# Scattering the routed rows with four 32-column products side by side instead of four accumulating 128-column products

## The reference, cut to what matters

```python
# L0 ffn, last step: each of 64 slots (16 experts x 4) of a group of 16 tokens goes back to the token that it was picked from
out = jnp.einsum('...besd,...btes->...btd', inter, perm)
# x = x + tanh(g_ffn[0]) * out
# L1 attention, one head, keys and values are ctx_1024
logits = jnp.einsum('bqd,bkd->bqk', q, k) * scale + mask * NEG
attn = jax.nn.softmax(logits, axis=-1)
out = jnp.einsum('bqk,bkd->bqd', attn, v)
# x = x + tanh(g_xattn[1]) * out, then the layer norms of the last feed-forward
```

## Time and profile before

| | us |
|---|---|
| median of 3 runs | 1633.4 (1632.84 to 1636.59) |
| span of the profiled execution | 1630.0 |
| TensorE busy | 1327.1 (81%) |
| VectorE busy | 1032.4 (63%) |
| ScalarE busy | 759.7 (47%) |
| GpSimd busy | 432.6 (27%) |

### The profile page before, as it was taken

The page is one execution under the profiler, slowest core; times in us unless marked ns, Lnnn a source line. Parts: engine busy times, 40 slices in busy tenths (PEclk is TensorE's granted clock), DMA queues, the critical chain, the costliest instruction groups (busy, mean ns, idle before and its releaser), DMA issues. The chain is left out here.

```text
span 1630.0 us, 24926 instructions
## 1 busy us (share of the span) xinstructions
PE 1327.1 (81%) x8930; PEld 934.2 (57%) x8930; DVE 1032.4 (63%) x2374; ACT 759.7 (47%) x1145; POOL 432.6 (27%) x435
## 2 busy tenths in 40 slices
PE   6999999999999738999957999996141799343996
PEld 5787888878888527666524666664041444142442
DVE  5577666766667533444334778786496399776774
ACT  3233333333333212665333555554383655386991
POOL 1233333333323310110012787866100000000011
PEclk9999999999999968999978999998555699755998
DMA  6111222111221158787589988860300177421973
GB/s 217 46 66 67 73 84 103 65 71 66 94 93 40 40 213 293 261 300 271 219 305 278 256 238 231 235 183 29 121 1 3 78 310 305 162 78 51 419 311 149
DMA packets 100406, 261.79 MB, mean 161 GB/s; under 512 B 11120, under 2 KB 22480, under 8 KB 93136
## 3 DMA queue, kind: packets, MB, share of 16 engines
q1 hardware_dynamic: 88704, 226.82, 40.1%
q0 software_dynamic: 8688, 32.51, 5.8%
q10 hardware_dynamic: 2912, 1.14, 0.3%
HBM read 155.32 MB, written 105.12 MB: 160 GB/s over the span
## 5 line engine op out<-in xcount | busy, mean ns | idle before, releaser
L1197 PE MATMUL p_s<-p_rows,p_permT 128*128 128x512 f32 x256 | 131.5, 611 | 5.9 <-DMA p_rows<-inter_d 3.9
L916 PEld LDWEIGHTS p_sel<-p_pick,p_xp 128*128 128x128 bf16 x1536 | 89.5, 100 | 55.5 <-issue 34.2
L916 PE MATMUL p_sel<-p_pick,p_xp 128*128 128x128 bf16 x1536 | 100.9, 224 | 21.9 <-DMA p_xp<-xparts 19.3
L2261 POOL DMA_DIRECT2D p_y<-residual x8 | 10.0, 1254 | 405.4 <-POOLq L113 342.9
L1928 PE MATMUL p_z<-qT,w1T 128*128 128x512 bf16 x512 | 113.3, 385 | 2.1 <-PEq L113 2.1
L1054 DVE COPY p_selT<-p_sel 128x512 f32<-128x512 f32 x64 | 44.2, 691 | 104.5 <-PE p_sel L916 104.5
L2285 PE MATMUL p_o<-w2T,p_Gq 128*128 128x512 bf16 x384 | 85.9, 384 | 8.0 <-DVE p_Gq L2342 8.0
L1987 DVE MAX8 cand<-hid 128x8 f32<-128x128 f32 x384 | 74.7, 276 | 25.1 <-ACT hid L1975 25.1
L1928 PEld LDWEIGHTS p_z<-qT,w1T 128*128 128x128 bf16 x512 | 50.6, 99 | 64.7 <-issue 5.7
L999 ACT ACTIVATE p_selT<-p_sel 128x512 f32<-128x512 f32 x64 | 38.2, 597 | 88.3 <-PE p_sel L916 88.3
L341 PE MATMUL p_M<-p_ctxTh,p_Wkh 128*128 128x256 f32 x256 | 76.0, 297 | 1.9 <-DVE p_Wkl L663 1.9
(11 more groups left out here) (335 smaller groups left out, 3935.3 us busy)
## 6 DMA issues: line engine op xcount, KB each, us to landing
inter_d<-p_stage SPq DMA_DIRECT2D x64, 512.0 KB, 4.1
p_rows<-inter_d SPq DMA_DIRECT2D x128, 256.0 KB, 5.5
activations<-hid SPq DMA_DIRECT2D x24, 1024.0 KB, 3.9
p_cin<-in_ctx_dram SPq DMA_DIRECT2D x32, 512.0 KB, 5.1
xparts<-p_parts SPq DMA_DIRECT2D x16, 768.0 KB, 3.2
hid<-activations SPq DMA_DIRECT2D x10, 1024.0 KB, 9.1
p_xp<-xparts SPq DMA_DIRECT2D x3, 3072.0 KB, 24.9
p_xin<-in_x_dram SPq DMA_DIRECT2D x16, 512.0 KB, 4.2
```

Of the source, the lines that this page charges most:

```text
L916: mm = pe.matmul(bsel[u % 2][:, k * P:(k + 1) * P], xp[:, c, tile, r, :], pick[sb % 2][:, tile, :, :].rearrange("p s g -> p (s g)"), start ...
L1197: mm = pe.matmul(bo[t][:, :], permT[b % 2][:, t, k, :], R[b % 2][:, t, k, :], start=(k == 0), stop=(k == NK - 1))
```

## The change

The rows are laid out over the 128 partitions as 2 groups x 64 slots. A tile has 4 such pairs of groups (index h), and pair h holds only rows that belong to the 32 tokens 32h to 32h+31. So one product of 128 rows by 32 columns writes the 32 token rows of pair h at once, without accumulation, into partitions 32h to 32h+31 of the bank; four products, h = 0 to 3, fill the bank. They use different 32-column strips of the array. A row piece in DRAM is still 2 KB.

permT shrinks from 4 x 128 to 128 columns per tile, and with it the GpSimd multiplies (512 to 128 columns), the transposes (8 to 2 a step) and ScalarE's copy (1024 to 256 columns). A mask with two columns, `mask2`, is made once by VectorE. The four DMAs of a tile become one of 1 MB. And TensorE's queue is written in another order.

```diff
-        rows = inter_d.rearrange("(n g) (k s) d -> n k s g d", g=GR, s=SK)
+        rows = inter_d.rearrange("(n h g) (s q) d -> n (g s) h (q d)", h=GR // GH, g=GH, q=ND)
...
-                for k in range(NK):
-                    sp.dma_start(R[b % 2][:, t, k, :], rows[b * NT + t, k]).then_inc(s[f"r_in{b % 2}{t}"], 16)
+                sp.dma_start(R[b % 2][:, t, :, :, :].rearrange("p h q d -> p h (q d)"), rows[b * NT + t]).then_inc(s[f"r_in{b % 2}{t}"], 16)
...
-                mm = pe.matmul(bo[t][:, :], permT[b % 2][:, t, k, :], R[b % 2][:, t, k, :], start=(k == 0), stop=(k == NK - 1))
-                if k == NK - 1:
+                for h in range(GR // GH):
+                    toks = slice(h * TH, (h + 1) * TH)
+                    mm = pe.matmul(bo[t][toks, :], permT[b % 2][:, t, q, toks], R[b % 2][:, t, h, q, :], start=(q == 0), stop=(q == ND - 1))
+                if q == ND - 1:
...
             for i in range(STEPS):
-                for k in range(NT * NK):
+                if live(i - 2):
+                    scores(i - 2, 1)
+                if i + 1 < B:
+                    turn_perm(i + 1)
+                for t in range(NT):
                     if i < B:
-                        scatter(i, k // NK, k % NK)
-                    if k == 0 and live(i - 2):
-                        scores(i - 2, 1)
-                    if k == 1 and i + 1 < B:
-                        turn_perm(i + 1)
-                    if k == 3 and live(i - 2):
-                        turn_e(i - 2)
+                        scatter(i, t, 0)
+                if live(i - 2):
+                    turn_e(i - 2)
...
```

More of the change, by code:

```diff
@@ L1071, in _ @@
                 layer_out(n)
-SK = 16
-NK = SL // SK
+GH = 2
+TH = P // 4
+ND = 1
 SEG = 128
@@ L1085, in phase2b3 @@
         sbt = lambda n, s, d=F32: es.enter_context(nc.sbuf_tensor("p3_" + n, s, d))
-        R = [sbt(f"rows{i}", [P, NT, NK, D]) for i in range(2)]
+        R = [sbt(f"rows{i}", [P, NT, GR // GH, ND, D]) for i in range(2)]
         xy = [sbt(f"xy{i}", [P, NT, D]) for i in range(XD)]
-        spread = [sbt(f"spread{i}", [P, NT, SL, GR], BF16) for i in range(2)]
-        permT = [sbt(f"permT{i}", [P, NT, NK, P]) for i in range(2)]
+        spread = [sbt(f"spread{i}", [P, NT, ND, GH, SL // ND], BF16) for i in range(2)]
+        permT = [sbt(f"permT{i}", [P, NT, ND, P]) for i in range(2)]
+        mask2 = sbt("mask2", [P, GH])
         ident, identb = sbt("ident", [P, P]), sbt("identb", [P, P], BF16)
@@ L1110, in phase2b3 @@
         bS, bP = ps("SE"), ps("P")
-        names = """const_in ident_in ln_in identb_done tanh_done spread_done turned permT_done scattered added
+        names = """const_in ident_in ln_in identb_done mask2_done tanh_done spread_done turned permT_done scattered added
             var1 rstd1 norm1 cT_full c_high c_low nT_full n_high n_low S_full S_taken soft exp e_full e_high e_low rz_done v_high v_low
@@ L1188, in _, with scatter @@
         def _(pe):
-            def scatter(b, t, k):
-                if t == 0 and k == 0:
+            def scatter(b, t, q):
+                if t == 0 and q == 0:
                     pe.wait_ge(s["permT_done"], b + 1)
-                if k == 0:
-                    pe.wait_ge(s[f"r_in{b % 2}{t}"], 16 * NK * (b // 2 + 1))
+                if q == 0:
+                    pe.wait_ge(s[f"r_in{b % 2}{t}"], 16 * (b // 2 + 1))
                     if b >= 1:
                         pe.wait_ge(s["added"], NT * (b - 1) + t + 1)
-                mm = pe.matmul(bo[t][:, :], permT[b % 2][:, t, k, :], R[b % 2][:, t, k, :], start=(k == 0), stop=(k == NK - 1))
-                if k == NK - 1:
+                for h in range(GR // GH):
+                    toks = slice(h * TH, (h + 1) * TH)
+                    mm = pe.matmul(bo[t][toks, :], permT[b % 2][:, t, q, toks], R[b % 2][:, t, h, q, :], start=(q == 0), stop=(q == ND - 1))
+                if q == ND - 1:
                     mm.then_inc(s["scattered"], 1)
@@ L1205, in turn_perm @@
                 for t in range(NT):
-                    for k in range(NK):
-                        mm = pe.transpose(bP[:, :].bitcast(BF16)[:, (t * NK + k) * P:(t * NK + k + 1) * P],
-                                          spread[b % 2][:, t, k * SK:(k + 1) * SK, :].rearrange("p s g -> p (s g)"), identb[:, :])
+                    for q in range(ND):
+                        mm = pe.transpose(bP[:, :].bitcast(BF16)[:, (t * ND + q) * P:(t * ND + q + 1) * P],
+                                          spread[b % 2][:, t, q, :, :].rearrange("p g s -> p (g s)"), identb[:, :])
                 mm.then_inc(s["turned"], 1)
@@ L1262, in _ @@
             for i in range(STEPS):
-                for k in range(NT * NK):
-                    if i < B:
-                        scatter(i, k // NK, k % NK)
-                    if k == 0 and live(i - 2):
-                        scores(i - 2, 1)
-                    if k == 1 and i + 1 < B:
-                        turn_perm(i + 1)
-                    if k == 3 and live(i - 2):
-                        turn_e(i - 2)
[L1272 to L1281, removed]
+                if live(i - 2):
[3 more added lines that the diff above has]
+                for t in range(NT):
+                    if i < B:
+                        scatter(i, t, 0)
+                if live(i - 2):
+                    turn_e(i - 2)
+                if live(i - 1):
+                    turn_xn(i - 1)
+                if live(i - 2):
+                    attend(i - 2, 0)
+                    attend(i - 2, 1)
+                if i < B:
+                    turn_ctx(i)
+                if live(i - 1):
+                    scores(i - 1, 0)
         @block.scalar
@@ L1289, in permT_out @@
                     act.wait_ge(s["scattered"], NT * (b - 1))
-                act.activation(permT[b % 2][:, :, :, :], bP[:, :].bitcast(BF16).rearrange("p (t k q) -> p t k q", t=NT, k=NK), ACT.Copy).then_inc(s["permT_done"], 1)
+                act.activation(permT[b % 2][:, :, :, :], bP[:, :].bitcast(BF16)[:, 0:NT * ND * P].rearrange("p (t q k) -> p t q k", t=NT, q=ND), ACT.Copy).then_inc(s["permT_done"], 1)
             def shifted(dst, src, rstd, minus, done, t):
@@ L1383, in spreads @@
                 for t in range(NT):
-                    v = pool.tensor_tensor(spread[b % 2][:, t, :, :],
-                                           perm[:, b * NT + t, :].rearrange("p (s a) -> p s a", a=1).broadcast_to([P, SL, GR]),
-                                           gmask[:, :].rearrange("p (a g) -> p a g", a=1).broadcast_to([P, SL, GR]), ALU.mult)
+                    v = pool.tensor_tensor(spread[b % 2][:, t, :, :, :],
+                                           perm[:, b * NT + t, :].rearrange("p (s a q) -> p q a s", a=1, q=ND).broadcast_to([P, ND, GH, SL // ND]),
+                                           mask2[:, :].rearrange("p (a g c) -> p a g c", a=1, c=1).broadcast_to([P, ND, GH, SL // ND]), ALU.mult)
                 v.then_inc(s["spread_done"], 1)
@@ L1420, in gains @@
                 pool.tensor_tensor(hid[:, b * NT:(b + 1) * NT, :], hh[:, :, :], of_all(lnb), ALU.add).then_inc(s["hid_done"], 1)
+            pool.wait_ge(s["mask2_done"], 1)
             spreads(0)
@@ L1512, in attended @@
                 dve.scalar_tensor_tensor(xy[b % XD][:, t, :], bO[t][:, :], rz[:, t:t + 1], xy[b % XD][:, t, :], ALU.mult, ALU.add).then_inc(s["x3_done"], 1)
+            dve.tensor_reduce(mask2[:, :], gmask[:, :].rearrange("p (h g) -> p g h", g=GH), AX.X, ALU.add).then_inc(s["mask2_done"], 1)
             dve.memset(mhalf[:, :], -0.5)
```

## The result

The changed kernel takes 1653.68 us (1651.58 to 1654.84, 4 runs) against 1634.88 us (1632.84 to 1636.59) of the kernel before: a ratio of 1.011, 95% interval 1.0096 to 1.0125. It is 18.8 us slower. The profiled execution has a span of 1652.3 us and a time of 1654.13.

What follows compares the result with a forecast made beforehand. Two bounds at once: TensorE's work (15.4 us a round) and a chain of 16.33 us. Slow rounds +24.5, others -0.3, start -4 gave span 1650.2, plus 3.4: 1654 us; likeliest 1645 to 1661, 8 in 10 1629 to 1662.

Steps and rivals of the forecast that it cites:

- The chain: Middle rounds: aggregation, GpSimd, ScalarE, VectorE, back to aggregation fill 16.33 us; no scatter product in it; 0.13 us gainable before `attended`.
- Products side by side: Scatter products on TensorE: four narrow ones run together, 0.9 us a tile, 1.8 a round instead of 6.96.
- The third rival: Scatter products don't run side by side; TensorE stays as busy, no pause, 1630 to 1635 us; 7%.
- The pause: TensorE, after the scatter products, stands idle about 5 us each round until the exponentials allow the transposes of e.
- Clock and port: Lower clock delays e's transposes 0.45 us; VectorE's small multiplication then waits for GpSimd: 2.23 us in 11 of 13 rounds.
- The first and second rivals: Clock stays up at e's transposes: 1628 us, 12%; VectorE's multiplication gets in ahead of GpSimd's instruction: 1634 us, 8%.
- What the low clock costs alone: Transposes of e at the lower clock: 0.45 us a round, held to be little by itself.
- The start: Before the first mark: earlier lnb, shorter spreads(2) and earlier first softmax save 4 us, between 1 and 6.
- The sum: Whole kernel: slow rounds +24.5, two others -0.3, start -4, so +20.2 us on the span, 1654 us.
- The last rival: TensorE was the bound after all; rounds fall to 13.5 us, time 1593 us; 5%.

Runs made afterwards that it cites:

- e2: Changed kernel plus 24 unused TensorE products per step between the scatter products and the transposes of e; 1619.23 us, ratio 0.9908.
- e1: Changed kernel with the two small instructions of `inverse` in the other order, multiplication before reciprocal; 1631.72 us, ratio 0.9975 to the kernel before.
- f5: Changed kernel plus 24 unused TensorE products per step, and `maxima` moved ahead of `e_low` on VectorE; 1601.45 us, ratio 0.9799.
- g1: Changed kernel plus 12 unused TensorE products per step ahead of the transposes of e; 1632.44 us, ratio 0.9985, profiled run 1622.84 us.

## Why the prediction was right, point by point

- **The chain.** As told. What has no place in it (eight scatter products, six transposes, GpSimd's and ScalarE's shorter instructions) gave nothing more in the middle; the high-clock run (e2) has rounds of 16.10, 0.23 below 16.33, where I had 0.13.
- **Products side by side.** A tile took 1.06 us with 0.2 of tail, near 0.87 (0.9 predicted). The third rival is out. TensorE's busy time is 12.7 us a round, not 10: at the low clock its other work lasts longer. In e2, at the full clock, it is 10.4 without the unused products.
- **The pause.** 4.92 us in the steady rounds ("about 5").
- **Clock and port.** In all thirteen rounds the multiplication took 2.4 us (11 predicted); a slow round is 18.56 us (18.54). Only the first is 17.00, 0.90 above its 16.10 of before: `maxima` is not in it. The first and second rivals are out in the plain kernel. The rule of the Trainium skill (TensorE: Matmul & The Clock Gate, HAM oscillation — how this bites in real kernels) on bursts and pauses, which would have it in every round, was right about the count: the transposes took 1.12 us in all thirteen.
- **What the low clock costs alone** was taken too small in the text ("would be little by itself"): e1 gives 0.82 us a round, the wait for attention products among it. In the changed kernel this is hidden behind the longer wait for GpSimd.
- **The start** was the term that was off: 8.2 us gained, 4 predicted, bounds 1 to 6. The mis-sized part is lnb: it landed 3.9 us earlier (22.25 instead of 26.14 us from the first load), where I had about 1, with the reason that the DMA engines were nearly full. They were, at a share of 0.94 and 247 GB/s up to that landing; in the changed kernel they moved 300 GB/s at a share of 0.85, so about the same bytes took less of their time. Whether that is the larger DMAs or their new pattern was not tested. spreads(2) took 0.76 us instead of 2.06, as predicted; the remaining 3.0 us, the 1.6 and 1.4 of the section on the result, stand against about 2. That there are no locks before the first mark was a misreading: L1484 at 887.94 us takes 1.11 us in the kernel before, and its like in the changed kernel 1.39, instead of 0.17. It is in both, 0.28 us apart, so the sum hardly feels it.
- **The sum.** Rounds +27.65 (+24.2 predicted), start -8.2 (-4), rest +0.1: +19.5 against +20.2. Two errors of opposite sign, 3.4 and 4.2 us, nearly cancel, and that is luck; the 1654 us is nearer to the 1653.7 than the working deserves. The 3.4 us between the span and the median of the runs was also not all outside the span: a run's time is 1.8 us above its span (1654.13 and 1652.3 here), and the rest may be the earlier phase, whose end moves by up to 3.4 us from profile to profile.
- **The last rival**, that TensorE was the bound after all, is half true, in a way that I hadn't written: it bound together with the chain. Only with both cut does the round fall (f5).

## What to carry to other kernels

Before taking work off a busy engine, follow the chain that returns to itself from round to round and add it up; if it is as long as the round, the work removed becomes a pause. A pause has a price of its own on TensorE (0.8 us a round here), and a delay of 0.5 us can cost a round 2.2 us where a small VectorE multiplication then meets a long GpSimd instruction: look where such an instruction stands against GpSimd's, and keep some tenths of a microsecond between them, or swap it with a neighbour. Narrow products paid here only in a block; spread out singly they cost more than full ones. And look at rounds in which one piece of work is missing: they show for nothing what taking it out is worth.

## What was not expected of the hardware

- The order of VectorE and GpSimd at the port is decided within hundredths: L1504, recorded 0.01 to 0.04 us ahead of L1422, lost, in each of thirteen rounds, for 2.4 us; e1's multiplication, 0.2 us earlier, never lost in these rounds. In g1's fourteenth round it is recorded 0.05 us ahead of GpSimd's instruction (1113.77 and 1113.82), 0.02 us after the end of the one before, and gets in, in 0.23 us. The reciprocal of the same two numbers (L1502, 0.16 us; L1499 before, 0.15 us) shows no such wait while GpSimd's multiplication by lng runs.
- A lone product on 32 columns costs about 0.31 us more than a full one of the same 512 columns.
- Twelve unused products in a round gave one run of 1622.8 us and ten from 1630.8 to 1634.4 us, 24 gave 1618.5 to 1620.7. What sets the one apart was not found: it is the only one of the eleven with a profile.
